# Graph attention layer: the table stage rebuilt block by block, with four-base products combined on VectorE and relation products as 32-row bands

## What is computed

```python
def _decomp(x, nt, w_comp, w_basis):          # 4 bases, mixed per node type
    W = (w_comp @ w_basis).reshape(8, 128, 128)
    return einsum('ni,tio->tno', x, W)[nt, arange(n)]
k, q, v = _decomp(x, node_type, ...) three times
kt = einsum('nhi,thij->tnhj', k, relation_att)[edge_type, src]
vt = einsum('nhi,thij->tnhj', v, relation_msg)[edge_type, src]
e  = (q[dst] * kt).sum(-1) * relation_pri[edge_type] * 0.25
a  = softmax of e over the edges of each destination
agg = segment_sum(a * vt, dst)
out = relu(_decomp(agg, node_type, ...) + x @ loop_weight + bias)
return layernorm(x + out)
```

## Time and profile before

| what | us |
|---|---|
| median of three runs | 2160.51 |
| lowest, highest | 2154.51, 2161.91 |
| span of the profiled execution, first to last instruction | 1543.8 |
| median less span | 616.7 |
| table stage, first projection to last product | 25.4 to 314.5 |
| first gather of the table | 320.1 |
| query stage | 314.5 to 375 |

### The profile page before, as it was taken

The page is one execution under the profiler, slowest core; times in us unless marked ns, Lnnn a source line. Parts: engine busy times, 40 slices in busy tenths (PEclk is TensorE's granted clock), DMA queues, the critical chain, the costliest instruction groups (busy, mean ns, idle before and its releaser), DMA issues.

```text
span 1543.8 us, 28784 instructions
## 1 busy us (share of the span) xinstructions
PE 1194.1 (77%) x6399; PEld 922.9 (60%) x6400; DVE 1026.4 (66%) x2684; ACT 704.7 (46%) x1849; POOL 954.6 (62%) x941
## 2 busy tenths in 40 slices
PE   6999999988777776767767767766777776666797
PEld 2444444445667665666656666655666765565697
DVE  5854444366787777667676766676676767666686
ACT  1222232255666554544554555555555445541143
POOL 3876000057577777777777777777777777772242
PEclk9999999999888888788887788888888778887699
DMA  4464445564333333333333333333333333332022
GB/s 117 192 242 172 195 184 197 217 200 128 88 107 105 109 106 106 104 106 106 107 106 106 106 106 100 105 104 106 106 104 105 106 107 106 105 104 60 7 79 60
DMA packets 93779, 184.27 MB, mean 119 GB/s; under 512 B 26359, under 2 KB 59624, under 8 KB 87408
## 3 DMA queue, kind: packets, MB, share of 16 engines
q0 software_dynamic: 41680, 113.71, 25.7%
q1 hardware_dynamic: 48352, 69.42, 12.4%
q10 hardware_dynamic: 3648, 0.14, 0.1%
HBM read 127.71 MB, written 56.26 MB: 119 GB/s over the span
## 4 chain that ended last, share of the span: by engine, by line
POOL 36%; PE 29%; issue 18%; DVE 9%; DMA 3%; DVEq 3%; ACT 1%; POOLq 0%; ACTq 0%; SPq 0%
POOL kv L1108 35%; PE pb L1426 9%; PE pb L1411 5%; PE pb L1665 3%; DVE agg L680 3%; PE pb L1570 2%; PE pb L1519 2%; DVEq L651 2%; PE pb L1648 1%; PE pb L1480 1%; DMA onehot<-in_x_dram 1%; PE pb L1389 1%; DVE kv L411 1%; DMA kv<-table,idx_now 1%; DVE work L645 1%
## 5 line engine op out<-in xcount | busy, mean ns | idle before, releaser
L1108 POOL DMA_INDIRECT kv<-table,idx_now x832 | 819.9, 985 | 441.1 <-issue 248.7
L1570 PE MATMUL pb<-work,onehot 128*128 128x136 f32 x1664 | 334.2, 333 | 108.6 <-DVE agg L680 74.0
L680 DVE TENSOR_TENSOR agg<-agg,pb 128x136 f32 x832 | 240.0, 289 | 199.0 <-issue 70.6
L1570 PEld LDWEIGHTS pb<-work,onehot 128*128 128x128 f32 x1664 | 274.9, 230 | 135.6 <-issue 82.9
L1262 ACT ACTIVATE work<-pb 128x512 f32<-128x512 f32 x208 | 124.0, 596 | 336.4 <-PE pb L1508 336.4
L1519 PE MATMUL pb<-q_all,work 128*128 x1664 | 270.9, 315 | 1.6 <-ACT work L1262 0.9
L1519 PEld LDWEIGHTS pb<-q_all,work 128*128 128x128 f32 x1664 | 247.3, 227 | 10.0 <-issue 8.8
L1250 ACT ACTIVATE work<-lane,neg_lane 128x128 f32<-128x128 f32 x800 | 253.0, 390 | 0.0
L537 DVE TENSOR_TENSOR work<-kv,pb 128x512 f32<-128x512 f32 x208 | 142.2, 684 | 104.5 <-DMA kv<-table,idx_now 71.4
L1508 PE MATMUL pb<-ident,onehot 128*128 128x128 f32 x832 | 155.8, 318 | 62.7 <-ACT onehot L1256 59.5
L1426 PE MATMUL pb<-onehot,kv 128*128 128x512 f32 x392 | 186.1, 592 | 0.0
(11 more groups left out here) (194 smaller groups left out, 1175.5 us busy)
## 6 DMA issues: line engine op xcount, KB each, us to landing
table<-kv SPq DMA_DIRECT2D x49, 1024.0 KB, 3.8
kv<-table,idx_now POOLq DMA_INDIRECT x832
seg<-item_bias SPq DMA_DIRECT2D x208, 16.0 KB
kv<-in_x_dram SPq DMA_DIRECT2D x8, 384.0 KB
onehot<-in_x_dram SPq DMA_DIRECT2D x7, 384.0 KB
kv<-in_x_dram SPq DMA_DIRECT2D x6, 448.0 KB, 3.7
out_dram<-kv SPq DMA_DIRECT2D x6, 448.0 KB
onehot<-tile_blocks POOLq DMA_DIRECT2D x1, 784.0 KB, 4.6
```

Source lines behind the costliest of these rows:

```text
L680: v.tensor_tensor(a, a, PB[banks[i // 2 % len(banks)]][:, (i % 2) * 256:(i % 2) * 256 + W], ALU.add).then_inc(s_added, 1)
L1108: pool.indirect_dma_start(out=kv[:, o:o + 2 * D], out_offset=None, in_=table, in_offset=bass.IndirectOffsetOnAxis(ap=idx_now[par][:, i:i + ...
L1570: mm = t_.matmul(PB[banks[k % len(banks)]][:, u * 256:u * 256 + W], onehot[:, o:o + P], wv[:, b % WR, h * 2 + u, :], start=True, stop=True)
```

## The change

All of it belongs to the table stage and to what runs beside it. In the diff below the parts stand in this order: sizes, DVE (`terms` and its loop), SP, ACT, PE.

- **Projection.** For each block, two products of 512 columns (x block times [k base 0, v base 0, k base 1, v base 1], then bases 2 and 3), as natural rows of nodes; DVE combines the four bases with the per-node coefficients, eight instructions of 128 columns per block (`terms`). The 16 spread products and 16 multiplications of a chunk go. The coefficients come from 7 tiny products per chunk with 16 columns each (`coefficients`).
- PE transposes k and v of each block (`turn_kv`), ACT copies both in one instruction of 256 columns (`copy_kvT`).
- **Relations.** `att` and `msg` keep only their 32-row bands: for each band of 32 rows one product of 256 columns (8 types of 32), K = 32, each band with a PSUM bank of its own: 8 products per block (`table_rows`). ACT copies all four banks, 512 columns each; only for the last block DVE takes two.
- Four store buffers (SLOTS) instead of two, two x and two node type buffers.
- The side chain's DVE steps are placed at fixed blocks (4, 8, 12 to 20, 24, 34 to 38). No loops are left in the table stage on PE, DVE, ACT and SP.
- The loads at the start are divided anew between the queues of SP and ACT; SP waits for the items, loads the first queries' x and the first indices ahead of the store of block 45 (before: ahead of the stores of the last chunk).

```diff
+    RW = 32
+    RG = D // RW
+    SLOTS = 4
...
-        Bk, Bv = [w1.take(NB * D).rearrange("p (b d) -> p b d", b=NB) for _ in range(2)]
+        Bkv = w1.take(NB * 2 * D).rearrange("p (b k d) -> p b k d", b=NB, k=2)
...
-        att = h1.take(T * D)
-        msg = h1.take(T * D)
+        att = h1.take(T * RW)
+        msg = h1.take(T * RW)
...
+        TILES_AT, STARTS_AT, BIAS_AT, QUERIES_AT = 4, 8, 24, BLOCKS - 4
+        COLUMNS_AT = [12, 13, 15, 16, 18, 19, 20]
+        ITEMS_AT = [34, 35, 37, 38]
...
+            def terms(n):
+                if n % CB == 0:
+                    dve.wait_ge(s_coef_copied, n // CB + 1)
+                after(dve, s_kv_turned, n - 1, 1, 0)
+                for b in range(NB):
+                    if b % 2 == 0:
+                        dve.wait_ge(s_projected, n * 2 + b // 2 + 1)
+                    for kind in range(2):
+                        o = kvn[:, n % 2, kind, :]
+                        of = PB[2 + b // 2][:, (b % 2 * 2 + kind) * D:(b % 2 * 2 + kind + 1) * D]
+                        c = coef_kv[:, (n * 2 + kind) * NB + b:(n * 2 + kind) * NB + b + 1]
+                        if b == 0:
+                            v.tensor_scalar(o, of, c, None, ALU.mult).then_inc(s_terms, 1)
+                        else:
+                            dve.wait_ge(s_terms, n * TERMS + 2 * (b - 1) + kind + 1)
+                            v.scalar_tensor_tensor(o, of, c, o, ALU.mult, ALU.add).then_inc(s_terms, 1)
...
+            for n_ in range(BLOCKS):
+                terms(n_)
+                if n_ == 0:
+                    scale_relations()
+                if n_ % CB == 2 and n_ // CB + 1 < CHUNKS:
+                    types(n_ // CB + 1)
...
+            for n in range(BLOCKS):
+                ch = n // CB + 2
+                if n % CB == 2 and ch < CHUNKS:
+                    x_chunk(ch)
+                    types_chunk(ch)
+                if n == QUERIES_AT:
+                    queries_in()
...
+                sp.wait_ge(s_table_copied, copied(n))
+                sp.dma_start(table[n * P * T:(n + 1) * P * T, :].rearrange("(p t) f -> p t f", t=T),
+                             stage[:, n % SLOTS, :, :]).then_inc(s_table_stored[n % SLOTS], 16)
...
+            for n in range(BLOCKS + 2):
+                ch, at = n // CB, n % CB
+                if n >= 3:
+                    copy_table(n - 3, 2)
+                    copy_table(n - 3, 3)
+                if 1 <= n <= BLOCKS:
+                    copy_kvT(n - 1)
...
+                if n >= 2:
+                    copy_table(n - 2, 0)
+                    copy_table(n - 2, 1)
...
+            def project(n, half):
...
+                after(pe, s_terms, n - 1, TERMS, NB * (half + 1))
+                t_.matmul(PB[2 + half][:, :], xT[:, c * P:(c + 1) * P],
+                          Bkv[:, 2 * half:2 * half + 2, :, :].rearrange("p b k d -> p (b k d)"),
+                          start=True, stop=True).then_inc(s_projected, 1)
+
+            def turn_kv(n):
+                pe.wait_ge(s_terms, n * TERMS + TERMS)
+                after(pe, s_kvT_copied, n, 1, 0)
+                for kind in range(2):
+                    mm = t_.transpose(PB[1][:, kind * P:(kind + 1) * P], kvn[:, n % 2, kind, :], ident[:, :])
+                mm.then_inc(s_kv_turned, 1)
+
+            def table_rows(n):
+                pe.wait_ge(s_kvT_copied, n + 1)
+                for kind, rel in enumerate((att, msg)):
+                    for g in range(RG):
+                        r = slice(g * RW, (g + 1) * RW)
+                        if kind == 0:
+                            after(pe, s_table_copied, n - 1, RG, g + 1)
+                        mm = t_.matmul(PB[4 + g][:, kind * T * RW:(kind + 1) * T * RW], kvT[r, n % 2, kind, :],
+                                       rel[r, :], start=True, stop=True)
+                        if kind == 1:
+                            mm.then_inc(s_table_product, 1)
...
+            for n in range(BLOCKS + 2):
+                ch, at = n // CB, n % CB
+                if n < BLOCKS:
+                    project(n, 0)
+                if 1 <= n <= BLOCKS:
+                    turn_kv(n - 1)
+                if n < BLOCKS:
+                    project(n, 1)
...
+                if n >= 2:
+                    table_rows(n - 2)
```

More of the change, by code:

```diff
@@ L375, in _ @@
             v = nc.vector
-            did(v.memset(comp, 0.0))
-            did(v.memset(ntype, -1), "comp_zero")
+            did(v.memset(comp, 0.0), "comp_zero")
+            did(v.memset(att, 0.0))
+            did(v.memset(msg, 0.0), "rel_zero")
+            for r in range(2):
+                did(v.memset(ntype[r], -1), f"types_zero{r}")
             did(v.memset(pad_rows[:, 0:P], NP - 1))
@@ L403, in scale_x @@
[L403 to L439, removed]
+                dve.wait_ge(s_node_types_loaded[ch % 2], ch // 2 * 48 + 48)
@@ L509, in combine @@
+            last = BLOCKS - 1
+            for g in range(2, RG):
+                dve.wait_ge(s_table_product, last * RG + g + 1)
+                after(dve, s_table_stored[last % SLOTS], last // SLOTS, 16, 0)
+                v.tensor_copy(stage_of(last, g), bank_of(g)).then_inc(s_table_split, 1)
             def combine(ch):
@@ new lines, in _ @@
+            x_chunk(0)
+            sp.wait_ge(s_setup, mark["comp_zero"])
+            for k in range(3):
+                for j, w in ((2, comp_a), (3, comp_q)):
+                    sp.dma_start(comp[32 * k:32 * k + T, j * NB:(j + 1) * NB], w).then_inc(s_comp_loaded, 16)
+            types_chunk(0)
+            for kind, w in enumerate((basis_k, basis_v)):
+                sp.dma_start(Bkv[:, :, kind, :], w.rearrange("b (i o) -> i b o", o=D)).then_inc(s_bases_loaded, 16)
+            sp.wait_ge(s_setup, mark["rel_zero"])
@@ new lines, in turn_items, with bank_free @@
+            def turn_items(i):
+                a, k0, k1 = ITEM_TURNS[i]
+                if i == 0:
+                    pe.wait_ge(s_lanes_rows, 1)
+                bank_free()
+                for k in range(k0, k1):
+                    t_.transpose(PB[0][:, (k - k0) * P:(k - k0 + 1) * P], (lanes, srcf)[a][:, k, :],
+                                 ident[:, :]).then_inc(s_items_turned, 1)
+                bank0.append((s_items_copied, a * IPR + k1))
+            bank0 = []
+            def bank_free():
+                if bank0:
+                    pe.wait_ge(*bank0[-1])
@@ L1435, in _ @@
             pe.wait_ge(s_const, 8)
-            turn_x(0)
+            turn_x(0, 0)
             pe.wait_ge(s_setup, mark["comp"])
-            for j in range(CO):
-                coefficient(0, j)
+            coefficients(0)
             pe.wait_ge(s_bases_loaded, 16 * 2)
-            projections(0)
-            pe.wait_ge(s_setup, mark["att"])
-            table(0)
-            projections(1)
-            table(1)
-            pe.wait_ge(s_lanes_rows, 1)
-            pe.wait_ge(s_table_keys, 2 * 2 * CB)
@@ L1449, in _ @@
-            pe.wait_ge(s_table_values, 2 * 2 * CB)
-            for a, (rows, bank) in enumerate(((lanes, 4), (srcf, 6))):
-                for k in range(IPR):
-                    t_.transpose(PB[bank + k // 4][:, k % 4 * P:(k % 4 + 1) * P], rows[:, k, :],
-                                 ident[:, :]).then_inc(s_items_turned, 1)
-            projections(2)
-            pe.wait_ge(s_items_copied, 2 * IPR)
-            table(2)
-            with pe.Fori(3, CHUNKS - 1) as ch:
-                projections(ch)
-                table(ch)
```

429 lines of the change are left out of this document (206 added, 223 removed).

## The result

| | median us (lowest to highest, runs) |
|---|---|
| kernel before | 2160.05 (2154.51 to 2161.91, 4) |
| changed kernel | 2039.50 (2035.06 to 2048.22, 4) |
| ratio | 0.9451, 95% interval 0.9424 to 0.9477 |

120.6 us less, where I forecast 94 less (2066). The page of the changed kernel comes first: span, busy time by engine, PE and its clock in 40 slices.

A forecast was written before the change was run, and what follows sets the result against it. PE bounds the table stage, on whose end all else hangs: 13 + 49 x 3.9 + 8 + 5 = 217 us to the last product, against 314.5; with SP's 3 us, 94 less, so 2160.5 - 94 = 2066 us, range 2018 to 2147.

The forecast's parts named there:

- I take it as fixed: Whole run: the 616.7 us by which the profiled span lies below the median stay unchanged, so 2160.5 - 94 = 2066.
- The hedge: Whole run: if all were stretched alike (2160.5 / 1543.8 = 1.40), 132 us would go, giving 2029; held by the range.
- the bands' 1.7 us: Table stage, PE: 16 band records per block, streaming side by side but loading one by one at 0.105 us each.
- rows 5: Profile rows of before: eight single-row f32 weight loads in a row take 0.96 us, used to price the bands' loads.
- the first rival: Table stage: bands and loads wholly side by side, ACT and PE's ring decides, 3.2 us per block, 2032 us; chance 0.19.
- The pace: Table stage: 3.9 us per block, from PE's 3.8 and 0.1 for changes between 128 rows and bands.
- side chain: DVE's extra steps in the table stage: seven columns about 0.7 us each, the other steps about 3 together; 8 us.
- The slower clock: Rival, table stage: PE's new waits bring the granted clock to 0.81, 39 us more, 2105 us; chance 0.13.
- first projection: Start of the table stage: first projection at 13 us in place of 25.37, since the 16 multiplications go; 12 us gained.
- rounds that run out: End of the table stage: two more pipeline rounds (terms, transposes, copy and bands) run out, about 5 us.
- last product to first gather: After the table stage: last copy and store as before, 5.5 us, plus 3 us for SP's queue; gathers at 226.
- my case's own: Range of the main forecast alone, 2047 to 2093 us (drains 0 to 0.56, bands 1.4 to 2.0); chance 0.43.

The follow-up runs named there:

- k128: Changed kernel with the eight relation products of a block over all 128 rows, zeros outside the band: 1532.81 us, 0.9907 of the kernel before on the same chip.
- after_again: The changed kernel, unedited, on a chip that gives the kernel before 1546 us: 1440.09 us, ratio 0.9314 to the kernel before.
- sp_order: Changed kernel with the first two groups' index and segment loads moved on SP's queue behind the last store: 1433.69 us, 0.9279 of the kernel before.
- cols_twice: Changed kernel with each of DVE's seven column sums issued twice: 1456.22 us, 0.9412 of the kernel before on the same chip.
- gather_late2: Changed kernel with POOL's first gather held until DVE's last query step, repeated on another chip: 1487.74 us, one run.

## Why the prediction was right and wrong

**The step that failed first: "I take it as fixed".** The 616.7 us between span and median were not time outside the span; own time less span is 1.8 us in every pair seen. The span came from a chip on which the program takes 1546 us, the median from one on which it takes 2160. The sum itself can therefore be held against 105.7 us, where the profile's condition was kept, and against 120.6, where it wasn't. The hedge (all stretched alike by 1.40, 132 us gained) is wrong in its mechanism too: the table stage is stretched little (the first gather comes at 216.85 instead of 207.98), the stages with gathers much (the edge stage 1630 us instead of 1105). That the change gains 14.9 us more there (120.6 less 105.7) isn't explained; there is no trace of before from such a chip. So it is in part luck that 2039.5 lies in my range: the gain was worked out from a span that doesn't belong to the time that it was taken from.

**The mis-sized term: the bands' 1.7 us.** They take 1.1, or 1.3 with the 0.2 behind them, for which I had 0.1. The step was "one by one in loading, because rows 5 are the only rows with few rows of the array in them". Rows 5 are loads into the same rows of the array; the 16 loads into four different bands come 0.04 apart. The sum by the 3.07 of the Trainium skill, which I had given to the first rival, was the right one, and k128 shows that the factor belongs to the 32 rows.

**The pace.** Quiet blocks take 3.21 to 3.27 us (1.06 + 0.22 + 0.86 + 1.1), and x and coefficients add 1.03 per chunk: 3.38 per block, against 3.9. PE is busy 156.6 of 160 us here and 160.0 of 160 in k128:

```profile
30.00:190.00 160.00, 156.62 (x1122) 82.45 (x1115) 122.29 (x413) 117.39 (x262) 90.96 (x69) 1.00 0.88 335
```

```profile
30.00:190.00 160.00, 160.00 (x694) 118.16 (x693) 83.85 (x266) 76.48 (x165) 85.05 (x68) 1.00 0.58 221
```

So the pace of the first rival came, 3.4 with the side chain for 3.2, but not by its mechanism: PE still sets it, and ACT waits for the bands 48 times (38.7 us in all), not PE for ACT. The slower clock didn't come in this stretch: 1.00; only the last bands, from 192.5 on, ran at a granted clock of 0.50.

**Term by term**, on the chip of after_again:

| term | forecast | measured |
|---|---|---|
| first projection | 13 | 16.5 |
| 49 blocks | 191 | 164.7 (49 x 3.235 + 6 x 1.03) |
| side chain | 8 | 3.4 |
| rounds that run out | 5 | 8.6 (the rest, to the end of the last product at 193.2) |
| last product to first gather | 9 | 14.8 |
| first gather | 226 | 208.0 |

So the 18 us by which the gather came early are 26 and 5 too much for the blocks and the side chain, and 13 too little for the other three, so misses the other way covered 13 of 31. The side chain's 3.4 is what is left of the 161.7 us between the first copy of the table (27.63) and the last of four (189.29), 47 blocks, after 152.0 for quiet blocks and 6.2 for the six chunks whose x and coefficients lie in between. I had counted each column's 0.7 over the spare; at single blocks it is seen (70.45 to 71.57 and after, in the chain), but PE makes most of it good. The rounds at the end cost more, since the last bands wait bank by bank for ACT's copies and the last of them run at the lower clock.

**The start.** I took away what the multiplications had taken and didn't count what ACT issues ahead of its first copy: 22 loads, until 14.5. **SP's queue.** The 21 issues take 12.4 us (182.41 to 194.85), not the 8.6 that I had at 0.41 each, and 3 us of it on the path was too little: sp_order brings the gather forward by 6.4. ACT waits for none of them, as I had it, but the stores do. **Four buffers.** I had used them only to say that ACT doesn't wait. That is right, and they are worth 13.7 us, in the main because a store at this pace takes 5.1 us and not the 2.6 to 3.8 of the earlier trace rows.

**What was right.** The table stage bounds the kernel, and its gain passes to the end nearly whole (105.7 of 111.5). PE stays the bound, DVE and ACT lie beneath it, the items come in time. 2039.5 lies in the range of 2018 to 2147, and outside my case's own 2047 to 2093; 2160.5 less the 105.7 of the profile's conditions would have been 2054.8, inside it.

## To carry to other kernels

When the span of a profile and the time of the runs lie hundreds of us apart, settle first whether they come from the same conditions; a sum made against such a span holds for the stages that the condition leaves alone, and no more. A product over zeros outside a block-diagonal band is worth cutting into row bands even for f32: the products overlap and the loads too, and after the cut look at the number of store buffers and at what stands ahead of the last stores in the queue, both of which were covered at the old pace. In cols_twice TensorE paid twice for standing some 2 us, once for the wait and once for the product at 1.2 GHz behind it, so for a long step of an engine that feeds it look at the granted clock too.

## What the runs showed that I had not expected

The same program takes 1440 us on some chips and 2040 on another, the kernel before 1546 and 2160. For the changed kernel the table stage is nearly alike, with a first gather at 207.98 and 216.85. From then on, while gathers run, other engines stand between their instructions: DVE's steps come 2.8 instead of 0.28 us apart, the queries end at 340 instead of 262 us, and the edge stage lasts 1630 instead of 1105. The first 64 gathers go as quickly, one every 1.25 us, and their bytes come at about 110 GB/s by the view of DMA; the 65th starts 155.8 us after the first (372.66) instead of 88.8, because POOL waits for DVE. The chain of waits cuts DVE's gaps into pieces of 0.70 us, by turns its own sequencer (DVEq) and "issue", and SP needs 0.70 us for each of the loads of x at 255 and 260, which take 0.38 to 0.40 from 214 us on in after_again. DVE's steps themselves keep their 0.35 us. That points at the sequencers and not at the engines, but no run tests it.

The gaps follow the gathers more than once in this trace. POOL issues none from 391.91 to 398.08 and none from 416.89 to 436.23. DVE's long gaps end some 4 us after the last gather of a batch (395.6 and 420.8) and come back some 6 us after the first of the next (404.0 and 442.2). The first pause in DVE's timeline:

```profile
395.59 0.30 DVE L708 TENSOR_TENSOR agg<-agg,pb 128x136 f32 x1 [6.73 <-remote]
...
402.33 0.29 DVE L708 TENSOR_TENSOR agg<-agg,pb 128x136 f32 x1 [0.17 <-issue]
...
408.12 0.30 DVE L708 TENSOR_TENSOR agg<-agg,pb 128x136 f32 x1 [4.09 <-remote]
```

The granted clock in the edge stage is 0.70 on average instead of 0.82, which fits a PE that stands more often. Whether a property of that chip does it, or the sharing of its memory or its DMA engines with something else, stays open: it was not met again on three further chips, and gather_late2, meant to tell it, ran on one of these. That the gaps come from the gathers rests on their place in one trace alone, and no run with the gathers moved shows it. Whether unrolled query loops help there wasn't tried either.
